# Layer-norm constants moved from VectorE to GpSimd, two ScalarE steps reordered and one PSUM bank for four products

## The reference, cut to what matters

```python
x = x + tanh(g_xattn) * xattn(ctx, ctx, layernorm(x), Wk, Wv, bv, Wq, bq, Wo, bo)
x = x + tanh(g_ffn)   * ffn(layernorm(x), w_gate, w_up, w_down)

def layernorm(x):          # over the 512 features of a token
    return (x - mean(x)) / sqrt(var(x) + 1e-5)
def xattn(k, v, q, ...):   # softmax((q Wq' + bq)(k Wk')' / sqrt(512)) (v Wv' + bv) Wo' + bo
def ffn(x, ...):           # quant(silu(quant(x) Wg') * (quant(x) Wu')) Wd', weights quantised too
```

## Time and profile before

| | |
|---|---|
| median of 3 runs | 844.69 us (844.58 to 844.76) |
| the profiled execution | 844.58 us |
| its span | 842.8 us |
| granted TensorE clock | 0.999 of full speed |
| TensorE busy | 833.4 us (99%) |
| VectorE busy | 718.2 us (85%) |
| ScalarE busy | 379.0 us (45%) |
| GpSimd busy | 370.3 us (44%) |

### The profile page before, as it was taken

The page is one execution under the profiler, slowest core; times in us unless marked ns, Lnnn a source line. Parts: engine busy times, 40 slices in busy tenths (PEclk is TensorE's granted clock), DMA queues, the critical chain, the costliest instruction groups (busy, mean ns, idle before and its releaser), DMA issues.

```text
span 842.8 us, 11581 instructions
## 1 busy us (share of the span) xinstructions
PE 833.4 (99%) x4175; PEld 424.4 (50%) x4175; DVE 718.2 (85%) x1174; ACT 379.0 (45%) x669; POOL 370.3 (44%) x284
## 2 busy tenths in 40 slices
PE   9999999999999999999999999999999999999998
PEld 5566556544554445444544444444544454444443
DVE  5997989898999999988897899889887999877753
ACT  3666485633544544534453445335532454233320
POOL 4495337345534344345434543444344434344321
PEclk9999999999999999999999999999999999999999
DMA  9723020054235215432452254324532343222222
GB/s 321 275 71 118 16 63 14 13 119 109 60 68 126 60 38 112 120 63 56 101 130 60 61 110 118 74 60 86 99 70 60 77 88 76 56 57 52 61 62 72
DMA packets 170529, 72.70 MB, mean 86 GB/s; under 512 B 154228, under 2 KB 155622, under 8 KB 170472
## 3 DMA queue, kind: packets, MB, share of 16 engines
q1 hardware_dynamic: 170471, 71.97, 35.7%
HBM read 22.76 MB, written 8.39 MB: 37 GB/s over the span
## 4 chain that ended last, share of the span: by engine, by line
PE 65%; DVE 3%; issue 2%; DMA 0%; POOL 0%; ACT 0%; SPq 0%; POOLq 0%
PE banks L1658 41%; PE banks L1782 22%; PE banks L1721 1%; PE banks L1747 1%; PE banks L1746 1%; DVE arena L1178 1%; DVE arena L1176 0%; DMA arena<-h_parts 0%; PE banks L1722 0%; POOL arena L570 0%; DVE ring L1375 0%; DVE scal L1263 0%; DVE h_parts L1370 0%; SPq L484 0%; ACT arena L714 0%
## 5 line engine op out<-in xcount | busy, mean ns | idle before, releaser
L1658 PE MATMUL banks<-wgu_hi,x_T 128*128 128x512 f16 (+1 forms) x1536 | 441.3, 361 | 0.0
L1658 PE MATMUL banks<-wgu_lo,x_T 128*128 128x512 f16 (+1 forms) x768 | 277.5, 361 | 0.0
L1782 PE MATMUL banks<-wd,arena 128*128 128x512 f16 x1056 | 233.8, 379 | 1.1 <-DVE ring L1304 0.6
L1658 PEld LDWEIGHTS banks<-wgu_hi,x_T 128*128 128x128 f16 x1536 | 150.2, 98 | 154.1 <-DVE ring L1351 0.7
L1782 PEld LDWEIGHTS banks<-wd,arena 128*128 128x128 f16 x1056 | 102.8, 98 | 123.1 <-issue 1.0
L570 POOL TENSOR_TENSOR arena<-arena,h_r 128x1024 f32<-128x1024 f32 (+1 forms) x60 | 91.5, 1525 | 129.6 <-DVE h_r L1130 129.6
L570 POOL TENSOR_TENSOR arena<-arena,h_s 128x1024 f32<-128x1024 f32 x64 | 90.6, 1416 | 76.5 <-DVE arena L1178 46.3
L1658 PEld LDWEIGHTS banks<-wgu_lo,x_T 128*128 128x128 f16 x768 | 75.1, 98 | 76.2 <-issue 1.0
L570 POOL TENSOR_TENSOR xwork<-xwork,x_s 128x512 f32<-128x512 f32 x32 | 33.9, 1058 | 166.8 <-DVE xwork L1178 166.8
L1351 DVE SCALAR_TENSOR_TENSOR arena<-arena,scal,banks 128x512 f32<-128x512 f32 (+1 forms) x90 | 62.7, 697 | 41.6 <-PE banks L1658 37.3
L871 ACT ACTIVATE arena<-banks,scal 128x512 f32<-128x512 f32 (+1 forms) x96 | 62.0, 646 | 66.5 <-PE banks L1658 65.9
(11 more groups left out here) (175 smaller groups left out, 973.8 us busy)
## 6 DMA issues: line engine op xcount, KB each, us to landing
ring<-in_x_dram SPq DMA_DIRECT2D x8, 1024.0 KB, 5.2
out_dram<-ring SPq DMA_DIRECT2D x32, 256.0 KB, 2.0
arena<-in_L_ffn_w_down_dram SPq DMA_DIRECT2D x4, 704.0 KB, 4.0
arena<-in_L_ffn_w_gate_dram SPq DMA_DIRECT2D x5, 512.0 KB, 9.6
arena<-in_L_ffn_w_up_dram SPq DMA_DIRECT2D x5, 512.0 KB, 9.8
ring<-in_L_xattn_Wk_dram SPq DMA_DIRECT2D x4, 256.0 KB, 5.8
ring<-in_L_xattn_Wq_dram SPq DMA_DIRECT2D x4, 256.0 KB, 7.2
wd<-in_ctx_dram SPq DMA_DIRECT2D x1, 1024.0 KB
```

Source lines behind the costliest of these rows:

```text
L1658: ended = e.matmul(at, l, r, start=(i == 0), stop=(i == len(terms) - 1))
L1782: ended = e.matmul(down_ps(t)[:, :], l, r, start=(k == 0 and i == 0), stop=(k == KH - 1 and i == 2))
```

## The change

The two small instructions that negate the mean and add LN_EPS move from VectorE to GpSimd, in both statistics steps; VectorE now signals GpSimd with its last `bn_aggr`. On ScalarE `x_apply(3)` goes ahead of `down_high(1)`, and in the loop `x_apply(t + 2)` goes ahead of `attention_part(t, "a4")`, which holds something on ScalarE in tile 4 alone: `xn_copy(2, 1)`. The value products of batch 2 all go to bank 5; before they took 5, 7, 5 and 7.

```diff
--- before.py
+++ after.py
@@ -322,7 +322,7 @@
             return KEYS_HALF * (1 if (b + 1) * KEYS <= HALF else 2)
 
         def value_bank(b, i):
-            return (5, 4)[i % 2] if b == 0 else (5, 7, 4, 5)[i] if b == 1 else (5, 7, 5, 7)[i] if b < CUT else (7, 5)[i % 2]
+            return (5, 4)[i % 2] if b == 0 else (5, 7, 4, 5)[i] if b == 1 else 5 if b < CUT else (7, 5)[i % 2]
 
         def rest_moves():
             return sum(len(list(value_moves(b))) for b in range(STACKED, NBATCH))
@@ -591,12 +591,18 @@
 
             def ln1(b):
                 w.wait_ge(ln1_mv, b + 1)
+                e.tensor_scalar(mv1[:, :, 1], mv1[:, :, 1], LN_EPS, None, ALU.add).then_inc(*step())
+                e.tensor_scalar(shift1[:, :], mv1[:, :, 0], -1.0, None, ALU.mult).then_inc(*step())
+                w.wait_ge(pool_step, step.n)
                 e.tensor_tensor(rstd1[:, :], mv1[:, :, 1], neg_half[:, :], ALU.pow).then_inc(*step())
                 w.wait_ge(pool_step, step.n)
                 e.tensor_tensor(shift1[:, :], shift1[:, :], rstd1[:, :], ALU.mult).then_inc(ln1_rstd, 1)
 
             def x_stats(t):
                 w.wait_ge(x_mv, t + 1)
+                e.tensor_scalar(mv2[:, 1:2], mv2[:, 1:2], LN_EPS, None, ALU.add).then_inc(*step())
+                e.tensor_scalar(shift2[:, :], mv2[:, 0:1], -1.0, None, ALU.mult).then_inc(*step())
+                w.wait_ge(pool_step, step.n)
                 e.tensor_tensor(rstd2[:, :], mv2[:, 1:2], neg_half[:, 0:1], ALU.pow).then_inc(*step())
                 w.wait_ge(pool_step, step.n)
                 e.tensor_tensor(shift2[:, :], shift2[:, :], rstd2[:, :], ALU.mult).then_inc(x_rstd, 1)
@@ -1043,8 +1049,8 @@
             attention_part(1, "a1")
             attention_part(1, "a2")
             down_squares(3)
+            x_apply(3)
             down_high(1)
-            x_apply(3)
             gate_silu(1, 1)
             down_low(1)
             down_high(2)
@@ -1107,9 +1113,9 @@
                 gate_silu(t, 2)
                 attention_part(t, "a3")
                 h_squares(t, 0)
-                attention_part(t, "a4")
                 if t + 2 < NT:
                     x_apply(t + 2)
+                attention_part(t, "a4")
                 attention_part(t, "d soft")
             h_squares(NT - 1, 1)
             h_high(NT - 1, 0)
@@ -1218,10 +1224,7 @@
                     e.bn_stats(stats1[:, i, :], x_tile(b * TILES + i)).then_inc(*step())
                 w.wait_ge(dve_step, step.n)
                 for i in range(TILES):
-                    e.bn_aggr(mv1[:, i, :], stats1[:, i, :]).then_inc(*step())
-                w.wait_ge(dve_step, step.n)
-                e.tensor_scalar(shift1[:, :], mv1[:, :, 0], -1.0, None, ALU.mult).then_inc(*step())
-                e.tensor_scalar(mv1[:, :, 1], mv1[:, :, 1], LN_EPS, None, ALU.add).then_inc(ln1_mv, 1)
+                    e.bn_aggr(mv1[:, i, :], stats1[:, i, :]).then_inc(*step() if i < TILES - 1 else (ln1_mv, 1))
 
             def softmax(b):
                 sc = att_ps[:, 0:TILES * KEYS].rearrange("p (i n) -> p i n", i=TILES)
@@ -1307,10 +1310,7 @@
                 w.wait_ge(x1_made, t + 1)
                 e.bn_stats(stats2[:, :], x_tile(t)).then_inc(*step())
                 w.wait_ge(dve_step, step.n)
-                e.bn_aggr(mv2[:, :], stats2[:, :]).then_inc(*step())
-                w.wait_ge(dve_step, step.n)
-                e.tensor_scalar(shift2[:, :], mv2[:, 0:1], -1.0, None, ALU.mult).then_inc(*step())
-                e.tensor_scalar(mv2[:, 1:2], mv2[:, 1:2], LN_EPS, None, ALU.add).then_inc(x_mv, 1)
+                e.bn_aggr(mv2[:, :], stats2[:, :]).then_inc(x_mv, 1)
 
             def x_scales(t):
                 if t > 0:
```

## The result

The changed kernel takes **849.90 us** (median of 5 executions, 848.83 to 850.18) against 844.58 for the kernel before on the same chip: ratio 1.0064, 95% interval 1.0049 to 1.0079. It is slower by 5.3 us. I had forecast 846.1 with a range to 848.3; both are missed. The profiled execution took 850.62 us around a span of 848.8, 6.0 more than before.

The account below looks back on a forecast made before the run. TensorE's own matmuls bound the kernel from 260 us on, so only holes before 280 us count. Batch 2's scores + 1.6, less 0.30 before 259.88, plus 0.15 for the bank: + 1.4 us, 846.1 us, range 843.9 to 848.3.

Parts of the forecast that it names:

- Place 1: x_apply(3) ahead of down_high(1), 136 us: the longer GpSimd chain delays normalisation and casts, cost 2.0 us.
- Rival A: At 136 us both added GpSimd instructions catch one gap: cost 0.5 us, total -0.1, 844.6 us; chance 0.22.
- Places 2 and 3: 174 and 208 to 221 us: VectorE's 384 column rounding goes before GpSimd's product, gaining 1.25 and 1.78 us.
- Rival B: At 174 and 208 us GpSimd's product still goes first, no gains: +2.5 to +4.1 us, 847.2 to 848.8; chance 0.3.
- Place 4: x_apply(6) ahead of xn_copy(2,1), 229 us: scores start 1.40 us behind x_rstd(6) at 228.67; a hole over 2 us.
- Bank 5: Fourth value product of batch 2, 277.68 us: waits for VectorE to empty the bank, 0.15 us, bounds 0 and 1.2.
- Before 259.88: TensorE's wait there for VectorE, which VectorE then meets in time: 0.30 us recovered.
- Net, unhindered: nothing to 0.1 us later: Each statistics step: two added GpSimd instructions, about 0.3 us, against VectorE's saved 0.25 to 0.28.
- the gap rule: Added GpSimd instructions must fit gaps between two VectorE instructions, or wait for the next, 1.2 to 1.6 us on.
- Tail: The end of the kernel, after TensorE's solid stream: as before, no change.
- rival C: Holes close, the cost at 136 us is nothing: x_rstd(6) at 226.3, end -1.1 to -2.9 us, 841.8 to 843.6; chance 0.08.

Follow-up runs that it names:

- e3: The kernel before with only x_apply(3) moved ahead of down_high(1); 844.60 us, ratio 0.9999.
- e6: The changed kernel with down_high(1) ahead of x_apply(3) again; 846.03 us, ratio 1.0032 against the kernel before.
- e4: The kernel before with only x_apply(t + 2) moved ahead of the a4 step; 847.29 us, ratio 1.0029.
- e5: The changed kernel with the old banks (5, 7, 5, 7) for batch 2's value products; 850.73 us, ratio 1.0066 against the kernel before.
- e8: The changed kernel with nine extra matmuls on TensorE just ahead of down_subtract(1); 850.17 us, ratio 1.0063 against the kernel before.
- e12: The kernel before with both new orders and bank 5, all constants left on VectorE; 848.05 us, ratio 1.0035.
- e11: The changed kernel with the constants back on VectorE from x_stats(6) and ln1(3) on; 847.46 us, ratio 1.0030 against the kernel before.
- e14: The changed kernel with the constants of x_stats(8) alone back on VectorE; 849.92 us, ratio 1.0062 against the kernel before.
- e1: The kernel before with only the mean and epsilon instructions moved to GpSimd, old orders and banks; 845.23 us, ratio 1.0007.
- e13: The kernel before with all constants on GpSimd except those of x_stats(7), old orders and banks; 842.65 us, ratio 0.9977.
- e9: The kernel before with the constants on GpSimd only up to x_stats(5) and ln1(2), old orders and banks; 841.98 us, ratio 0.9967.

## Why the prediction was wrong

Point by point, in its own steps.

- **Place 1**: right. 2.0 forecast; 1.90 measured at the subtraction, 2.35 behind it. The path through the gaps came as written, product at 140.15 (forecast about 139.8). Rival A is refuted: the second instruction never shared a gap, here or at 175 and 228 us. e3 shows the order alone costs nothing; e6 shows what it costs once the constants are on GpSimd: 2.8 us between executions at full clock.
- **Places 2 and 3**: right in kind, 0.82 of 1.25 and 1.47 of 1.78. Rival B is refuted. No row has the 174.15 at which VectorE was to be ready: the rounding before ends at 174.35 and the long one is issued at 174.38.
- **Place 4**: right in kind. The scores start 1.37 behind x_rstd(6), forecast 1.40. But that came at 231.45 and not 228.67. The 2.78 us between are 1.68 of clock, 0.30 of place 1, 0.74 of gains at places 2 and 3 that were smaller, and 0.06 of the chain.
- **A term that was missing**: I took every TensorE hole at its own length, so the clock stood at nothing in the sum. In the changed kernel's trace it fell behind one of them, place 1, and cost 1.68 us; in e4, e5, e8 and e12 it fell behind place 4, 1.64 to 1.69 us. The kernel before has no hole over 1.24 us in this stretch and its clock stays at 1.00, so its rows had nothing from which to price it; that a hole of 2 us is a case outside them I should have said, with a bound.
- **Bank 5**: a step that failed in its mechanism. I took 0.15 within 0 and 1.2; it is 1.64, beyond its bound. The argument (TensorE comes later, VectorE doesn't) is right with the late constants on VectorE: e11 and e12 have no wait. With them on GpSimd, VectorE is held as far back as TensorE. x_stats(8) has a part in it (e14: 0.6 instead of 1.4); that x_stats(7) has the rest is read from the trace, for no run takes it back alone from the changed kernel.
- **Before 259.88**: 0.61 recovered instead of 0.30. From the matmul before to this one it took 0.68 us before and 0.31 now, so the wait was worth 0.37; two smaller ones, before 236.63 and 254.13, gave 0.09 and 0.14.
- **"Net, unhindered: nothing to 0.1 us later"**: the step that failed first, and the root of the bank's error as far as the traces show it. I applied the gap rule at places 1 to 4 and not at the steps that were unhindered before. x_stats(7) was one: two free instructions, 0.4 us of work, moved power and product behind 2.4 us of roundings. e1 against e13 prices this one step at 2.6 us between medians, with old orders and banks: 1.5 at full clock, the rest the lower clock behind the new wait. The Trainium skill's rule that I weighed for place 4 ("SBUF — State Buffer", Who interferes with whom) bears on this step too, and the rows at 247.28 and 247.32 agree with it.
- **Tail**: 0.6 us in the profiled execution (SP's last transposes take longer, and TensorE waits 1.15 for them instead of 0.55); the other changed kernels' traces show this wait at 0.4 to 0.5, so it is that execution's.
- **Small slips of the working**: rival A less half a microsecond is 844.1, not the 843.9 of the range, and rival C's 226.3 is the three old holes taken off 229.20, where its own terms give 226.6. Neither touches the forecast.

The account of the forecast: 1.6 - 0.30 + 0.15 = 1.45 forecast, 4.36 - 0.61 + 1.64 = 5.39 measured. Of the 3.9 us between them 1.7 are the clock, 1.5 the bank, 0.7 the smaller gains at places 2 and 3, 0.3 place 1, and - 0.3 the larger recovery before 259.88. By experiments on the medians: orders and bank 3.2 (e12), early constants with them - 0.6 (e11), late constants 2.7.

## What to carry to other kernels

Moving small instructions to GpSimd is judged also at every place where its chain was free before, not only where it was blocked: here the blocked chains of 174 and 208 us won 1.6 us on VectorE, and the free one of 249 us lost 2.2 (ScalarE's wait for it went from 3.24 to 5.43). Ask it per step, and move only the steps that win: e9 gains 2.9 us where all of them together gain nothing (e1, + 0.7 in the median, not told from no change). A hole of TensorE's near 2 us should be priced with what follows it, and waits in one stretch replace each other, so undoing one of several tells little until all are seen.

## What was not expected of the hardware

- A GpSimd instruction with a constant on 128x1 costs 0.21 to 0.24 us when free, the next starts 0.08 later; the port added up to 1.22 to it (1.44 at 135.53).
- The clock falls behind a hole in some executions of one kernel and not in others: of e1's eleven five have a mean clock of 0.997 to 0.998 and six of 1.00, 845.9 us and more against 845.2 and less. And the same hole of 2.5 us at place 4 is followed by 1.00 in the changed kernel and by 0.66 in e8.
- Up to 184 us identical instruction streams differ by 1.3 us between executions (e1, e9, e13), nearly the size of the whole change that I had forecast.
